# A decoder layer on one core: two more projection groups in rounded products, values by way of DRAM, and a reordered opening

## What is computed

```python
x = x + attn(layernorm(x))    # 32 query heads, 8 key/value heads, D = 64, rotary, causal, window of 32 back
x = x + xattn(layernorm(x))   # 16 heads of 16, keys and values from ctx_512[:, :256] (causal, so only those count)
x = x + ffn(layernorm(x))     # silu(x Wg) * (x Wu), of each 4 neighbours the 2 largest kept, then W_down

q = (x @ wq.T).reshape(B, S, 32, 64); k = ... (8 heads); v = (x @ wv.T).reshape(B, S, 8, 64)
q, k = q * cos + rotate_half(q) * sin, k * cos + rotate_half(k) * sin
attn = softmax(where(masked, -inf, q @ k.T / 8)); out = (attn @ v) @ wo.T
```

## Time and profile before

| | us |
|---|---|
| median of 3 runs | 407.32 |
| profiled execution | 407.13 |
| its span, first to last instruction | 405.3 |
| TensorE matmul busy | 387.9 (96%) |
| TensorE weight load busy | 317.4 (78%) |
| VectorE busy | 289.1 (71%) |
| ScalarE busy | 214.3 (53%) |
| GpSimd busy | 169.5 (42%) |

### The profile page before, as it was taken

How to read it: one execution, slowest core, us unless ns; L and a number is a source line. 1 busy time by engine, 2 the same in 40 slices (tenths; PEclk the granted TensorE clock), 3 DMA queues, 4 the chain that set the end, 5 groups by cost and what they waited for, 6 DMA issues and landing times.

```text
span 405.3 us, 8287 instructions
## 1 busy us (share of the span) xinstructions
PE 387.9 (96%) x3064; PEld 317.4 (78%) x3064; DVE 289.1 (71%) x626; ACT 214.3 (53%) x547; POOL 169.5 (42%) x168
## 2 busy tenths in 40 slices
PE   8998899889999999999999999999999999999997
PEld 7667777767789877877789877887879778876795
DVE  4985932779849976588967987288876984586375
ACT  1573844297444653186634664167734756188331
POOL 5562697667710440157730350057832430057000
PEclk9998999999999999999999999999999999999999
DMA  7995340213000400243000220234000500200000
GB/s 205 362 342 155 105 132 10 97 52 79 23 15 0 153 5 0 85 124 86 16 13 2 93 67 0 79 99 104 2 0 2 157 2 1 81 0 2 27 0 27
DMA packets 33191, 28.40 MB, mean 70 GB/s; under 512 B 18688, under 2 KB 28032, under 8 KB 32896
## 3 DMA queue, kind: packets, MB, share of 16 engines
q1 hardware_dynamic: 33152, 27.87, 22.5%
HBM read 18.95 MB, written 4.98 MB: 59 GB/s over the span
## 4 chain that ended last, share of the span: by engine, by line
PE 55%; DVE 22%; issue 8%; POOL 8%; ACT 7%; POOLq 0%; DVEq 0%; ACTq 0%
PE ps L663 13%; PE ps L744 7%; PE ps L603 5%; DVE rope L982 4%; POOL prob L1290 4%; ACT prob L1429 4%; PE ps L529 3%; PE ps L538 3%; PE ps L624 3%; DVE mx L1012 3%; DVE total L1026 3%; PE ps L760 2%; DVE rope L979 2%; PE ps L562 2%; PE ps L702 2%
## 5 line engine op out<-in xcount | busy, mean ns | idle before, releaser
L1290 POOL TENSOR_TENSOR prob<-prob,inv 128x512 f32<-128x512 f32 x80 | 82.7, 1041 | 82.8 <-DVE inv L1032 82.8
L1429 ACT ACTIVATE prob<-ps,mx 128x128 f32<-128x128 f32 (+1 forms) x128 | 52.6, 429 | 16.3 <-DVE mx L1010 13.2
L663 PE MATMUL ps<-wo_sb,qs 128*128 128x256 f32 x256 | 59.8, 380 | 0.0
L1283 POOL TENSOR_TENSOR qs<-rope 128x512 f32<-128x512 f32 x32 | 40.8, 1277 | 41.6 <-DVE rope L982 37.7
L603 PE MATMUL ps<-ident_sb,prob 128*128 128x128 f32 x320 | 49.8, 278 | 5.0 <-POOL prob L1290 4.5
L663 PEld LDWEIGHTS ps<-wo_sb,qs 128*128 128x128 f32 x256 | 46.8, 190 | 6.8 <-issue 1.6
L1439 ACT ACTIVATE pT<-ps 128x512 f32<-128x512 f32 x76 | 45.6, 600 | 10.6 <-PE ps L603 9.9
L982 DVE TENSOR_TENSOR rope<-ps,trig_sb 64x512 f32<-64x512 f32 x70 | 48.2, 688 | 0.9
L603 PEld LDWEIGHTS ps<-ident_sb,prob 128*128 128x128 f32 x320 | 36.6, 141 | 14.0 <-POOL prob L1290 10.0
L1266 POOL TENSOR_TENSOR rstd<-vareps,power 128x1 f32<-128x1 f32 x24 | 13.2, 553 | 67.0 <-DVE vareps L961 66.6
L1010 DVE TENSOR_REDUCE mx<-ps 128x2 f32<-128x512 f32 (+1 forms) x48 | 32.7, 689 | 9.0 <-PE ps L583 8.2
(11 more groups left out here) (169 smaller groups left out, 800.6 us busy)
## 6 DMA issues: line engine op xcount, KB each, us to landing
k<-kx SPq DMA_DIRECT2D x32, 128.0 KB, 2.9
q<-qx SPq DMA_DIRECT2D x28, 128.0 KB, 2.5
vb<-v_sb SPq DMA_DIRECT2D x42, 64.0 KB, 2.1
work<-in_wgu SPq DMA_DIRECT2D x4, 512.0 KB, 8.5
wo_sb<-in_wo SPq DMA_DIRECT2D x1, 2048.0 KB, 15.1
vb<-v_sb SPq DMA_DIRECT2D x36, 32.0 KB, 3.0
wq_raw<-in_wqk SPq DMA_DIRECT2D x2, 512.0 KB, 8.2
wd_sb<-in_wd SPq DMA_DIRECT2D x1, 1024.0 KB, 5.5
```

The source lines that it names most:

```text
L663: mm = pe.matmul(half_banks(use, b)[:, 0, :], window_o[t][:, pair, r, :], wo_sb[:, pair, r, :], start=(pair == 0 and r == 0), stop=(pair = ...
L1283: pool.tensor_tensor(to, cos, sin, ALU.add).then_inc(s_sums, 1)
L1290: pool.tensor_tensor(p, p, inv[:, i % ND, 0:g].unsqueeze(2).broadcast_to([P, g, 512 // g]), ALU.mult).then_inc(s_norm, 1)
L1429: ins = act.activation(prob[:, i % ND, h * k:(h + 1) * k], ps[:, BANK_S + i % 2, h * k:(h + 1) * k], ACT.Exp, bias=mx[:, i % ND, h:h + 1], ...
```

## The change

It has four parts. (1) `SPLIT` gets q1 and q2, which are made in rounded products in b = 1 and b = 2 only; in b = 0 they stay plain. Their weights are rounded and split in the window stage of b = 1. (2) Values are copied to `pT` (once to `xn`), stored to DRAM (`vx`), and loaded from there into `vb` by four transfers of 256-float rows for a pair of tiles or a tile. (3) The opening: v0 comes after q7; the swapped halves are written to PSUM banks 0 to 4 and not to SBUF; the sum of q7 is made on VectorE; units 0 and 1 come before the latent values and unit 2 before the latent keys. (4) Only four of the eight `round_weights` stay in the opening, the others go to units 3 to 6 of b = 0, and the first two `half_weights` from units 3 and 4 to units 7 and 8; `keys_rest` comes after unit 2 in b = 0.

```diff
+V0_AFTER = 7
+ROUNDED = 4
-SPLIT = (3, 4, 5, 6, 7, 8, 9)
+SPLIT = (1, 2, 3, 4, 5, 6, 7, 8, 9)
+LATER = (1, 2)
-V_BLOCKS = 16 * 2 * 2 * (P // QB)
+V_BLOCKS = 16 * 4
-NEXT_USES = [("ln1", 0), ("k0", 1), ("k1", 2), ("q0", 0), ("q1", 1), ("q2", 2), ("q3", 0), ("v0", 1), ("q4", 2), ("q5", 0),
-             ("q6", 1), ("q7", 2), ("v1", 0), ("xv", 1), ("xk", 2)]
+NEXT_USES = [("ln1", 0), ("k0", 1), ("k1", 2), ("q0", 0), ("q1", 1), ("q2", 2), ("q3", 0), ("q4", 1), ("q5", 2), ("q6", 0),
+             ("q7", 1), ("v0", 2), ("v1", 0), ("xv", 1), ("xk", 2)]
-        swaps = dict(zip(SWAPPED, (prob[:, 1], prob[:, 2], prob[:, 3], pT[:, 0], pT[:, 1])))
+        swaps = {g: ps[:, n, :] for n, g in enumerate(SWAPPED)}
+        def v_home(b, t):
+            w = xn[:].rearrange("p t d -> p (t d)") if b == 0 and t else pT[:, t]
+            return w.rearrange("p (e c d) -> p e c d", e=2, d=HD)
...
+            def v_out(b, t):
+                wait_drained(sp, f"v{t}", b)
+                sp.dma_start(vx[v_batch(b), t], v_home(b, t).rearrange("p e c d -> p (e c d)")).then_inc(s_vx, 16)
+            def v_blocks(b, tiles, done):
+                first, last = (t * (P // QB) for t in tiles)
+                sp.wait_ge(s_vx, 16 * v_count(b, tiles[1] - 1))
+                for e in range(2):
+                    src = vx[v_batch(b)].rearrange("t (j s) (e n) -> e s (t j) n", s=QB, e=2)[e]
                     for own in range(2):
+                        to, end = 64 * e + WIN * (1 - own), min(last, NQB - own)
+                        sp.dma_start(vb[to:to + QB, first + own:end + own].rearrange("p j c d -> p j (c d)"),
+                                     src[:, first:end]).then_inc(done, 16)
...
             sp.wait_ge(s_zero, 2)
+            v_out(None, 0)
             v_blocks(None, (0, 1), s_vfirst)
             sp.dma_start(wd_sb[:], wd).then_inc(s_wd, 16)
-            v_blocks(None, (1, TT))
+            v_out(None, 1)
+            v_blocks(None, (1, TT), s_vb)
...
                 for t in range(TT if b + 1 < B else 1):
+                    if b + 1 < B and (b or t == 0):
+                        v_out(b, t)
                     cross_queries(b, t)
                 if b + 1 < B:
-                    v_blocks(b)
+                    if b == 0:
+                        v_out(b, 1)
+                    v_blocks(b, (0, TT), s_vb)
...
-                    if b is not None and g in SPLIT:
+                    if b is not None and g in SPLIT and (b or g not in LATER):
...
-                if g == QG // 2 - 1:
+                if g == V0_AFTER:
                     pe.wait_ge(s_wv, 16)
                     v_tile("v0", None, 0)
             v_tile("v1", None, 1)
+            pe.wait_ge(s_cbf, 2)
+            pe.wait_ge(s_zero, 2)
+            unit_scores(0, 0)
+            unit_scores(0, 1)
             pe.wait_ge(s_xkv, 16 * 2)
             latent_values(None, 1)
+            unit_scores(0, 2)
             latent_keys(None)
...
-                dve.tensor_tensor(t[:, 0], half_banks(name, b), trig_sb[:, 0:1, :].broadcast_to([P, 2, S]), ALU.mult)\
-                   .then_inc(drained(name, b), 1)
+                dve.tensor_tensor(t[:, 0], half_banks(name, b), trig_sb[:, 0:1, :].broadcast_to([P, 2, S]), ALU.mult)
                 dve.tensor_tensor(t[:, 1], other, trig_sb[:, 1:2, :].broadcast_to([P, 2, S]), ALU.mult)\
-                   .then_inc(s_swapped, 1)
+                   .then_inc(drained(name, b), 1)
...
-                    if i == 1:
+                    if i == (1 if b else HEAD - 1):
                         keys_rest(prior)
...
                 (rope_swapped if g in SWAPPED else rope_group)(f"q{g}", None, GROUPS + g + 1)
+                if g == QG - 1:
+                    wait_drained(dve, f"q{g}", None)
+                    dve.wait_ge(s_sums, GROUPS + g)
+                    to, cos, sin = rope_terms(f"q{g}", GROUPS + g + 1)
+                    dve.tensor_tensor(to, cos, sin, ALU.add).then_inc(s_sums, 1)
...
                     unit_norm(b, i)
+                    if b == 1 and NQB - len(LATER) <= i:
+                        if i == NQB - len(LATER):
+                            wait_filled(pool, f"q{LATER[-1]}", 0)
+                        rest_of_weights(len(SPLIT) - NQB + i)
...
                 if u >= NPT:
                     act.wait_ge(s_av, u - NPT + 1)
+                if b == 0 and i < TT:
+                    act.wait_ge(s_vx, 16 * v_count(None, i))
+                elif b + 1 < B and NQB <= i < NQB + (TT if b else 1):
+                    act.wait_ge(s_vx, 16 * v_count(b, i - NQB))
                 act.activation(pT[:, i % NPT, :], ps[:, BANK_PT + i % 2, :], ACT.Copy).then_inc(s_pT, 1)
...
-                    if b == 0 and HEAD <= i < HEAD + EARLY_SPLIT:
-                        half_weights(i - HEAD)
+                    if b == 0 and HEAD <= i < HEAD + WCHUNKS - ROUNDED:
+                        round_weights(ROUNDED + i - HEAD)
+                    elif b == 0 and i < HEAD + WCHUNKS - ROUNDED + EARLY_SPLIT:
+                        half_weights(i - HEAD - (WCHUNKS - ROUNDED))
+                    elif b == 1 and i < HEAD + len(LATER):
+                        half_weights(len(SPLIT) - len(LATER) + i - HEAD)
...
-            for c in range(WCHUNKS):
+            for c in range(ROUNDED):
+                if c == ROUNDED // 2 and V0_AFTER not in SWAPPED:
+                    v_copy("v0", None, 0)
                 round_weights(c)
+            v_copy("v1", None, 1)
             act.wait_ge(s_ident, 16)
             act.activation(minus_bf[:], ident_sb[:], ACT.Copy, scale=-1.0).then_inc(s_minus, 1)
-            v_copy("v1", None, 1)
+            unit_exp(0, 0)
             act.wait_ge(s_zero, 2)
             latent_values(None)
-            unit_exp(0, 0)
+            unit_exp(0, 1)
             latent_keys(None)
-            for i in range(1, HEAD):
-                unit_exp(0, i)
+            unit_exp(0, 2)
```

More of the change, by code:

```diff
@@ L51 @@
 SWAPPED = (2, 3, 4, 5, 6)
+V0_AFTER = 7
+ROUNDED = 4
 UNITS = NQB + XU
-SPLIT = (3, 4, 5, 6, 7, 8, 9)
-SPLIT_ORDER = [g for g in SPLIT if g >= QG] + [g for g in SPLIT if g < QG]
+SPLIT = (1, 2, 3, 4, 5, 6, 7, 8, 9)
+LATER = (1, 2)
+SPLIT_ORDER = [g for g in SPLIT if g >= QG] + [g for g in SPLIT if g < QG and g not in LATER] + list(LATER)
 EARLY_SPLIT = 2
@@ L350, in weights, with v_batch, v_count, rope_terms @@
             return wqk_sb[:, :, at:at + n]
+        def v_batch(b):
+            return 0 if b is None else b + 1
+        def v_count(b, t):
+            return TT * v_batch(b) + t + 1
+        def v_home(b, t):
+            w = xn[:].rearrange("p t d -> p (t d)") if b == 0 and t else pT[:, t]
+            return w.rearrange("p (e c d) -> p e c d", e=2, d=HD)
+        def rope_terms(name, n):
+            g = int(name[1:])
+            t = rope[:, (n - 1) % 2]
+            if name[0] == "q":
+                return qs[:, 2 * (g // R):2 * (g // R) + 2, :, g % R, :], \
+                    *(t[:, k].rearrange("p c (u s) -> p c u s", s=QB) for k in (0, 1))
+            return t[:, 0], t[:, 0], t[:, 1]
         def before(b):
@@ L624, in unit_values @@
                         mm = pe.matmul(ps[at:at + 64, BANK_O + e, p // 2 * P:(p // 2 + 1) * P],
[L625 removed]
+                                       vb[half, i, p, :], pT_i[half, p, :],
                                        start=True, stop=True, skip_group_check=True)
@@ L1269, in rope_sums @@
             def rope_sums(name, b, n):
-                g = int(name[1:])
-                if b is None and name[0] == "q" and g in SWAPPED:
-                    pool.wait_ge(s_swapped, SWAPPED.index(g) + 1)
-                else:
-                    wait_drained(pool, name, b)
-                t = rope[:, (n - 1) % 2]
-                if name[0] == "q":
-                    to = qs[:, 2 * (g // R):2 * (g // R) + 2, :, g % R, :]
-                    cos, sin = (t[:, k].rearrange("p c (u s) -> p c u s", s=QB) for k in (0, 1))
-                else:
-                    to = cos = t[:, 0]
-                    sin = t[:, 1]
+                wait_drained(pool, name, b)
+                to, cos, sin = rope_terms(name, n)
                 pool.tensor_tensor(to, cos, sin, ALU.add).then_inc(s_sums, 1)
@@ L1330, in batch @@
                         split_weights(c)
-                    for k in range(EARLY_SPLIT, len(SPLIT) - 1):
+                    for k in range(EARLY_SPLIT, len(SPLIT) - len(LATER) - 1):
                         rest_of_weights(k)
@@ L1361, in _ @@
                 rope_sums(f"k{g}", None, g + 1)
-            for g in range(QG):
+            for g in range(QG - 1):
                 rope_sums(f"q{g}", None, GROUPS + g + 1)
@@ L1386, in v_copy @@
                 wait_filled(act, name, b)
-                act.activation(v_sb[:, t, :], bank(name, b), ACT.Copy).then_inc(drained(name, b), 1)
+                act.activation(v_home(b, t), bank(name, b).rearrange("p (c e d) -> p e c d", e=2, d=HD), ACT.Copy)\
```

(3 more changed lines are left out.)

38 lines of the change are left out of this document (10 added, 28 removed).

## The result

The changed kernel took 402.50 us (median of 4 runs, 402.36 to 402.69) and the kernel before 407.03 beside it (4 runs, 406.22 to 407.41): a ratio of 0.9892, with a 95% interval of 0.9874 to 0.9909. The profiled execution took 402.36, its span is 400.6. The forecast was 402.7, and 402.5 before the 0.19 for the median was added.

A forecast was written before the change was run, and what follows sets the result against it. TensorE was taken as the bound nearly throughout, except the opening's rotary chain on VectorE and GpSimd and the half-clock first units. Opening 4.2 plus rounding 0.4 gave 4.6 off 407.13: 402.5, plus 0.19 is 402.7; range 401.3 to 404.7.

The forecast's parts named there:

- Unit 0 at 29.1: Opening: the shorter rotary chain lets unit 0 begin at 29.1 instead of 31.93, 2.8 us earlier.
- Maxima at 30.4 and 31.8: First units of b = 0: full clock and closer units put the second maximum at 31.8 instead of 35.98, 4.2 us earlier.
- the median is 0.19 above it: Whole kernel: the median run lies 0.19 us above the profiled execution, turning 402.5 into 402.7.
- ScalarE's rounds and copies at nothing, 0.5 at most: Units 3 to 6 of b = 0: ScalarE's four moved rounds cost nothing, 0.5 us at most if one wait goes over.
- Values at 0: Value transfers by way of DRAM: no gain or loss; bounds 0 and 1.5 us in the opening.
- v0 loads landed by 36, first values at 38.5; v1's store about 38.7: Opening's value transfers: v0's loads have 2.5 us spare; v1's store lets the second pT copy go 0.8 late.
- The use and not the copy is late first: Opening, second copy to pT: its 0.8 us delay costs 0, since TensorE uses it only 2 us after.
- Rival (b): Opening: v1's store holds ScalarE and the exponentials, 1.5 us of the gain goes, 404.2; chance 0.10.
- Rounding 0.4, q1 nothing, q2 0.2 each: Cross stages of b = 1 and b = 2: rounded q2 saves 0.2 us each, q1 nothing; bounds 0 and 1.2.
- Remainders in b = 1 at 0.1 taken as 0: Window stage of b = 1: two GpSimd remainders hide under VectorE's wait for ScalarE; up to 2.6 us without it.
- Rival (a): First units meet half clock again; only 2.8 us of the opening's gain remain, 404.1; chance 0.15.
- Rival (c): Opening: v0's store queues behind the weights, first values 6.8 us later than in the kernel before, 411; chance 0.05.

The follow-up runs named there:

- rounds_in_opening: Changed kernel with all eight weight roundings in the opening and the first two half_weights at units 3 and 4, as before; 402.67 us, 0.9906 of the kernel before.
- values_alone: Kernel before with only the values sent by way of DRAM, stored from v_sb; 406.56 us against 406.36, ratio 0.9999.
- opening_alone: Changed kernel with the old SBUF-to-SBUF value transfers and q1 and q2 plain; 404.75 us against 406.36 for the kernel before, ratio 0.9963.
- q7_swapped: Changed kernel with q7 swapped too, which also moves v0's copy ahead of ScalarE's four rounds and v1's behind; 402.83 us, 0.9910 of the kernel before.
- plain_q1: Changed kernel with q1 plain and its weights unprepared, q2 still rounded; 402.47 us, 0.9904 of the kernel before.
- plain_q1q2: Changed kernel with q1 and q2 plain in all batches and their weights unprepared; 403.25 us against 406.36 for the kernel before, ratio 0.9918.
- two_more_gpsimd: Changed kernel with two more GpSimd subtractions, results unused, behind the last remainder of b = 1; 404.00 us against 406.56 for the kernel before, ratio 0.9935.

## Why the forecast held, point by point

- **Unit 0 at 29.1**: 29.19. The forecast's own terms (28.15 + 0.1 + 0.69 + 0.26) add up to 29.2; 29.1 was a slip of 0.1. The terms held one by one, as forecast and (measured): the second swapped instruction 0.68 (0.68), q6's end 26.05 (26.20), q7's end 28.15 (28.21), the sum 0.69 (0.69), v0 and v1 hidden. Between the sum's end and the mask stood 0.26, as assumed.
- **Maxima at 30.4 and 31.8**: 30.49 and 31.83. The fourth at 36.7: 36.65. The first units are worth 4.15 as reckoned. But this was reckoned against one kind of execution. Of the 4.15, 1.06 by the medians and up to 1.4 by the traces is the half clock, which the kernel before has in 15 of 58 runs; I read the earlier trace rows as a property of the kernel. What fails there is "the median is 0.19 above it": the profiled run was at 0.996, and the 406.74 to 407.41 then at hand reach up to such times, so the size of the gain against most executions is 3.8 and not 4.6. The changed kernel's time was not touched by that.
- **ScalarE's rounds and copies at nothing, 0.5 at most**: at nothing (rounds_in_opening: the same time within the intervals).
- **Values at 0**: right for the changed kernel, and only half right as a statement. By itself the route is neutral (values_alone); beside the early units the old one would have cost 1.5 (opening_alone). The sum came out since it was made for the whole; for the opening alone the same sum would have been 1.5 too low. The sign was in the earlier trace rows: 14 transfers take 8.95 to issue, so 16 begun at 28 end at 38, when the first values are wanted at 38.5 and still have to land.
- **v0 loads landed by 36, first values at 38.5; v1's store about 38.7**: values at 38.01; the store by 38.97, 0.2 us before its copy was due. "The use and not the copy is late first" did not have to be tried there, as the copy was not late. It was in q7_swapped, and the chain did lose: 1.39 of 1.64 reached TensorE's values, and 0.85 the first output. Rival (b) at 0.10 with 1.5 was a fair price. The Trainium skill ("DMA: Bandwidth & Descriptors", anatomy of one DMA) gives a fixed cost of about 2 us, which it measured on transfers issued by GpSimd. Here, from SyncE, the stores took 2.5 us in the median, but 5.8 and 6.6 when `wd_sb` had been issued just ahead, so in these traces what stands ahead decides.
- **Rounding 0.4, q1 nothing, q2 0.2 each**: q1 nothing (plain_q1, and 0.26 that became 0.59); q2 0.33 in b = 1 and 0.28 in b = 2, so 0.6 in the traces (0.78 between the times of plain_q1q2 and plain_q1). The term was undersized by 0.2: I took the 1.73 of a row of groups as the plain price, where this one stands alone and takes the 1.83.
- **Remainders in b = 1 at 0.1 taken as 0**: 0. The wait that covers them was the right one; it is now used up (two_more_gpsimd).
- **Rival (a)**, half clock again: not in any of 4 runs. It is no empty case, as opening_alone, with the same order on TensorE, was at 0.996 once in 12. **Rival (b)** did not come in the changed kernel's trace, with 0.2 us to spare. **Rival (c)**, the store of v0 behind the weights: it landed in 2.6 us. The queue was nearly empty by then, as argued, but not quite: `xwo_sb`, issued at 15.61, took 14.1 us and so landed at 29.7, after the store was issued at 27.76, and the store landed 0.7 behind it.

At the end stand 4.16 for the opening where 4.2 was said, and 0.61 for the rounding where 0.4 was said: 4.77 in all against 4.6.

## What to carry to other kernels

Before you price a clock dip or a stall from one profile, look whether every timed run has it: the mean granted clock beside each time tells that at once. When a change makes consumers earlier, price the unchanged transfers against the new due times too: a route that is neutral alone can be what lets the rest through. And when a step of a serial chain is shortened, count every member of that kind in the chain, not the last one.

## What the runs showed of the hardware

- The same program had a mean granted clock of 0.996 in 15 of 58 executions and of 0.999 or 1.000 in the rest; in its profile at 0.996 it is a stretch of 3.4 us at half clock. It stands behind pauses of TensorE: with these filled, 12 of 12 executions had full clock.
- A VectorE instruction with both inputs in SBUF that began during a GpSimd sum ended 0.54 to 0.55 us after that sum, in nine of nine cases (0.86 to 1.37 us long), and took 0.68 with GpSimd idle, at the same 128x512. With one input in PSUM it took 0.68 beside the sums too. The Trainium skill ("GPSIMD Engine Reference", specifications) names the shared interfaces and the contention of instructions with two SBUF inputs; the traces agree. The last sum, with two SBUF inputs and GpSimd idle, took 0.69.
- A 256 KB store to DRAM landed in 2.5 us in the median, in 5.8 and 6.6 with 1 MB issued 0.5 us ahead of it, and in 2.8 with that load moved behind it. Sixteen SBUF-to-SBUF transfers took SyncE 10.41 us to issue, 0.65 each.
- The opening starts up to 0.5 us apart between profiles of kernels that are alike up to there (the rotary step of q0 at 13.77 to 14.32), which is the size of the smaller effects above.
